# One branch per unit over two written-out sides, in place of one branch per pair of tiles

## What is computed

```python
x = x + _L0_conv_ref(_gn(x), w0, w1, w2, bias)     # wavelet convolution, three levels
x = x + _L1_conv_ref(_gn(x), spatial_weight)       # similarity filter
```

```python
patches = _extract_patches(x)                      # 25 neighbours of each point
dot = jnp.einsum('bchw,bckhw->bkhw', x, patches)
norm_x = jnp.sqrt(jnp.sum(x * x, axis=1))
norm_p = jnp.sqrt(jnp.sum(patches * patches, axis=1))
sim = dot / jnp.maximum(norm_x[:, None] * norm_p, 1e-08)
weight = (sim + 1.0) * 0.5 * spatial_weight[None, :, None, None]
out = jnp.einsum('bckhw,bkhw->bchw', patches, weight)
```

## Time and profile before

| | |
|---|---|
| median of three runs | 2016.01 us |
| the profiled execution: its time / its span | 2011.4 us / 2009.7 us |
| TensorE, matmul busy | 1638.6 us, 82% |
| VectorE busy | 1370.1 us, 68% |
| ScalarE busy | 748.9 us, 37% |
| GpSimd busy | 428.0 us, 21% |
| mean granted TensorE clock | 0.908 |
| one loop iteration (six between first and last L1529 branch) | 225.6 us |

### The profile page before, as it was taken

One profiled execution on the slowest core, in us unless ns is written; L12 is line 12 of the kernel. 1 busy time (PEld: TensorE's weight loads), 2 busy tenths in 40 slices (PEclk: granted clock), 3 DMA queues, 4 the chain that ended last, 5 costly groups with the idle time before them and its releaser, 6 DMA issues.

```text
span 2009.7 us, 52625 instructions
## 1 busy us (share of the span) xinstructions
PE 1638.6 (82%) x19071; PEld 899.9 (45%) x19071; DVE 1370.1 (68%) x1995; ACT 748.9 (37%) x1318; POOL 428.0 (21%) x760
## 2 busy tenths in 40 slices
PE   4868688888888888888888888888888889886587
PEld 3533244444544454444544454444544444443355
DVE  6434956885588756885588656884589666885554
ACT  1321134432444244432544234432444244432551
POOL 2344232212040222212040222212040222210000
PEclk8889889889998999889999889999999998898567
DMA  5233137754475627754575627754575637662665
GB/s 182 84 97 98 52 93 202 199 152 119 131 212 155 155 83 204 195 157 115 133 209 150 154 74 204 201 155 119 134 204 156 154 96 197 188 162 68 163 170 133
DMA packets 108623, 296.77 MB, mean 148 GB/s; under 512 B 24180, under 2 KB 57972, under 8 KB 107764
## 3 DMA queue, kind: packets, MB, share of 16 engines
q1 hardware_dynamic: 71408, 190.49, 36.1%
q0 software_dynamic: 36864, 101.47, 17.5%
HBM read 221.92 MB, written 69.94 MB: 145 GB/s over the span
## 4 chain that ended last, share of the span: by engine, by line
PE 56%; DVE 21%; issue 14%; ACT 4%; DVEq 2%; DMA 1%; POOL 1%; ACTq 0%; SPq 0%; POOLq 0%
PE conv L1272 14%; PE conv L1246 10%; PE gram L1337 7%; PE out_ps L1373 5%; PE stat_ps L1295 5%; PE conv L1231 5%; DVE wgt L1014 3%; PE out_ps L1362 3%; PE vals_ps L1320 3%; DVE st_s L965 2%; DVE eo L830 2%; DVE st_a L962 2%; PE conv L1493 2%; DVE st_v L976 1%; DVE st_b L957 1%
## 5 line engine op out<-in xcount | busy, mean ns | idle before, releaser
L1272 PE MATMUL conv<-thl,wconv 128*128 128x496 f16 (+2 forms) x1920 | 521.7, 398 | 29.5 <-issue 14.9
L1014 DVE SCALAR_TENSOR_TENSOR wgt<-gram,tapw 124x512 f32<-124x512 f32 x512 | 349.7, 685 | 269.0 <-PE gram L1337 232.8
L452 POOL DMA_DIRECT2D ring<-in_x x576 | 331.9, 582 | 354.2 <-ACT xa L524 263.9
L1337 PE MATMUL gram<-unit_mem 128*60 128x128 f16 x4096 | 251.5, 246 | 63.9 <-DVE wgt L1014 32.6
L1337 PEld LDWEIGHTS gram<-unit_mem 128*60 128x60 f16 x4096 | 151.2, 112 | 290.6 <-issue 289.8
L1246 PE MATMUL conv<-thl,wconv 128*128 128x480 f16 (+7 forms) x1200 | 257.7, 369 | 0.0
L1272 PEld LDWEIGHTS conv<-thl,wconv 128*128 128x128 f16 x1920 | 163.6, 101 | 197.8 <-issue 42.0
L481 POOL DMA_DIRECT2D up<-d_z x128 | 69.3, 546 | 666.1 <-DVE xa L945 630.6
L1295 PE MATMUL stat_ps<-st_sq,sq_c 128*128 128x306 f32 x256 | 112.2, 525 | 111.6 <-DVE flag L995 68.9
L524 ACT ACTIVATE vals<-vals_ps 124x512 f32<-124x512 f32 x128 | 76.2, 595 | 308.1 <-PE vals_ps L1320 307.5
L524 ACT ACTIVATE thl<-tw 128x1024 f16<-128x1024 f32 x64 | 67.7, 1058 | 329.1 <-DVE tw L830 184.2
(11 more groups left out here) (140 smaller groups left out, 2114.0 us busy)
## 6 DMA issues: line engine op xcount, KB each, us to landing
unit_mem<-d_hl SPq DMA_DIRECT2D x128, 360.0 KB
unit_mem<-d_hl SPq DMA_DIRECT2D x256, 180.0 KB
ring<-in_x POOLq DMA_DIRECT2D x288, 128.0 KB, 2.7
ring<-in_x POOLq DMA_DIRECT2D x288, 127.0 KB, 2.7
d_hl<-st_hl SPq DMA_DIRECT2D x64, 360.0 KB
d_v<-st_v SPq DMA_DIRECT2D x64, 360.0 KB
unit_mem<-d_v SPq DMA_DIRECT2D x64, 360.0 KB
up<-d_z POOLq DMA_DIRECT2D x160, 128.0 KB, 2.6
```

Of the source, the lines that this page charges most:

```text
L452: pool.dma_start(dst, src).then_inc(raw_in[slot], 16)
L1014: V.scalar_tensor_tensor(out=dst, in0=g, scalar=SIM_SCALE ** 2, in1=tapw[:, :].unsqueeze(1).to_broadcast([KN, 2, 2 * QN]), op0=ALU.add, op ...
L1272: last = mm(dst[:, :, b0:b1], wconv0[:, w, 2 * (p % ROWS4) + s, dx + 2, :], thl[:, p % 2, d, s, :, b0 + dx:b1 + dx] if p % ROWS4 != 1 else ...
L1337: last = mm(bank[row:row + KQ, col:col + QN], key[:, q, e_at, TH * KW * g:TH * KW * g + KQ], tile[:, :, TH * g + 1:TH * g + 1 + TH, 1:1 + ...
```

## The change

On both engines the body of a unit becomes a function `unit(j, guarded)`. In place of a branch in every pair there is one branch after the load of the flag, with the whole unit written out on each side: first the side with the guard in all eight pairs, then the side without any. `Chain.mark` and `Chain.back` let both sides use the same link numbers. On TensorE the wait for the flag and its load stand ahead of `conv_points` now, and so ahead of that function's own waits, where they stood in hook k = 0 behind them.

```diff
-            def weights(b, u, k, short_ones):
+            def weights(b, u, k, guarded):
...
-                with dve.If(short_ones > 0):
-
+                if guarded:
                     V.tensor_scalar(dst, guard_ps[0:KN, :].rearrange("p (t n) -> p t n", t=2), 1 / EPS_SIM, 1.0, ALU.mult, ALU.min)
                     dve.drain()
                     V.tensor_tensor(g, g, dst, ALU.mult)
                     dve.drain()
...
+                for j in range(CONV_TILES):
+                    if ls:
+                        dve.wait_ge(flag_done, START + 8 * b + j + 1)
+                        alone(dve)
+                        short_ones = dve.value_load(flag[0:1, j % FLAGS:j % FLAGS + 1], min_val=0, max_val=P * FN)
+                        chains = gn1_chain, gn2_chain, prep_chain, wino_chain
+                        marks = [chain.mark() for chain in chains]
+                        with dve.If(short_ones > 0):
+                            unit(j, True)
+                        for chain, mark in zip(chains, marks):
+                            chain.back(mark)
+                        with dve.Else():
+                            unit(j, False)
+                    else:
+                        unit(j, False)
...
-            def gram(b, u, k, short_ones):
+            def gram(b, u, k, guarded):
...
-                with pe.If(short_ones > 0):
-
+                if guarded:
                     pe.wait_ge(wgt_done, START + n)
...
                             if k == 0:
-                                pe.wait_ge(flag_done, START + 8 * b + j + 1)
-                                alone(pe)
-                                short_ones[0] = pe.value_load(flag[0:1, j % FLAGS:j % FLAGS + 1], min_val=0, max_val=P * FN)
                                 unit_here(b, j)
...
+                for j in range(CONV_TILES):
+                    if ls:
+                        pe.wait_ge(flag_done, START + 8 * b + j + 1)
+                        alone(pe)
+                        short_ones = pe.value_load(flag[0:1, j % FLAGS:j % FLAGS + 1], min_val=0, max_val=P * FN)
+                        with pe.If(short_ones > 0):
+                            unit(j, True)
+                        with pe.Else():
+                            unit(j, False)
+                    else:
+                        unit(j, False)
```

More of the change, by code:

```diff
@@ L146, in round, with mark, back @@
         self.base, self.k = n * self.per_round, 0
+    def mark(self):
+        return self.base, self.k
+    def back(self, mark):
+        self.base, self.k = mark
     def link(self, engine, instruction):
@@ L1069, in iteration, with unit @@
                     level1_out(i, 1)
-                short_ones = None
-                for j in range(CONV_TILES):
+                def unit(j, guarded):
                     h = j + AHEAD
[L1073 to L1076, removed]
                     for k in range(PAIRS):
@@ L1080, in iteration @@
                                 set_flag(b, 2)
-                            weights(b, j, k, short_ones)
+                            weights(b, j, k, guarded)
                             if k == 0 and j in (2, 3, 4, 5):
@@ L1378, in iteration @@
                 b = i - 1
-                short_ones = [None]
                 if conv_on:
@@ L1425, in iteration, with unit, hook @@
                         hook_1(n)
-                for j in range(CONV_TILES):
-                    def hook(n, j=j):
+                def unit(j, guarded):
+                    def hook(n):
                         if n not in HOOKS:
@@ L1441, in hook @@
                             if k < PAIRS:
-                                gram(b, j, k, short_ones[0])
+                                gram(b, j, k, guarded)
                             if k == 1:
```

## The result

The change takes 2213.24 us in the median of 4 runs (2198.08 to 2225.87), the kernel before 2020.41 (1999.98 to 2024.87, 4 runs). The ratio is 1.0973, with a 95% interval of 1.0869 to 1.1077: slower by some 10%. The forecast was 2140 us with a range of 2030 to 2205. The direction was right, and so was the main mechanism, the far jump of TensorE that has to wait for its target; the loss is 193 us where 129 were forecast, and 2213 lies outside the range. The profiled execution of the change took 2198.08 us, 186.7 more than that of before; what follows is about these 187.

A forecast was written before the change was run, and what follows sets the result against it. TensorE (82% busy) set the pace in units 6, 7 and the last iteration, waiting for VectorE's flag at other starts. Terms 79 + 50 + 40 + 10 - 35 - 15 = +129 on 2011.4 gave 2140 us, range 2030 to 2205.

The forecast's parts named there:

- the first rival: TensorE's jump target is already fetched, so a far jump costs what a pair's branch does: 1961 us; chance 0.08.
- Terms 5 and 6: TensorE's late instruction packets get rarer in denser straight code, -35 us; the removed pair branches save exposed hand-over time, -15 us.
- the fourth rival: Straight code is worth more: all late packets vanish, hand-overs give 46 us, jumps cost 2.5 with slack: 1960 us; chance 0.03.
- Term 8: VectorE's new branch over 69 to 105 instructions: zero cost, covered by TensorE's own jump; uncovered up to 2.5 us a unit.
- term 7: TensorE's flag wait and load (302 ns) moved ahead of `conv_points`' waits: zero, up to 0.3 us a unit where those last.
- The third rival: Both engines pay in turn: VectorE's jump also needs a packet, starting its first pair 2.5 us later: 2230 us; chance 0.05.
- the slack case: VectorE catches up within units 0 to 5 and no clock is lost anew, so only 22 starts count: 2027 us; chance 0.12.
- The packets: Sign in the instruction queue: some 270 packets in all instead of 236, as every unit ends with one fetched and dropped.
- term 2: Units 0 to 5 of seven iterations, 42 starts: TensorE 1.6 us late beyond its existing wait, three quarters counted, +50 us.
- the 3.6 us for every start: Idle added per TensorE far jump, priced like the loop's way back; 22 starts at TensorE's pace made +79 us.
- Term 3: TensorE's clock drops after idle: 14 starts of units 6 and 7 lose 2 us each, 42 others some 0.3; +40 us.
- Term 4: Where the plain side begins near a packet's end, TensorE wants the next at once: two of eight starts, +10 us.

## Why the prediction failed, point by point

**What held.** The target isn't there and has to be fetched: 64 of 64 branches over 3.3 us, so the first rival fell, and with it what I had read out of the 2048 instructions that the Trainium skill's page "Runtime: NRT & Kernel Launch" gives TensorE. In rows: 121 instructions jumped over cost 0.2 to 0.6 us, 401 cost 3.4 to 6.3 in six units of eight, and in one of the other two, unit 7, the same idle came a few instructions behind a short branch. The same section of the Trainium skill, "Instruction fetch mechanics", has blocks of 256 instructions and a stall where the target is outside the current two; the traces agree with it (the rows of before gave about 235 instructions for a packet), and give the price that it leaves open.

**Terms 5 and 6** (late packets -35, removed branches -15): idle by "issue" other than before first products fell by 36 us, and the kernel with short sides is 54 us faster than before, where the two terms had 50 together. Right; the fourth rival had 106 for them. **Term 8** (VectorE's jump 0) and **term 7** (load ahead 0): VectorE's branch is 56 ns in all 64, and the early load by itself moved nothing that can be seen. Right, and not only by the cover that I named for it: with VectorE's sides alone there is no jump of TensorE, and the kernel gains. The third rival is out, and so is the slack case: VectorE's longer waits (+204 us) went with a longer iteration.

**The packets**: 283 for some 270. Right.

**The step that failed is term 2, in unit 0, and with it the 3.6 us for every start.** To see it, the forecast has to be laid out by place. The starts of units 0 to 5 had 1.6 x 3/4 + 0.3 = 1.5 us each, those of units 6 and 7 3.6 + 2 = 5.6, those of the last iteration 3.6; the -40 of terms 4 to 6 spread over 64 units takes 0.6 from each. That makes, in us over the whole run:

| place | forecast | measured |
|---|---|---|
| unit 0, 7 times | 6 | 55 |
| units 1 to 5, 35 times | 30 | 49 |
| units 6 and 7, 14 times | 70 | 58 |
| last iteration, 8 times | 24 | 25 |
| sum | 130 | 187 |

49 of the 57 us missing are in unit 0. Three things were wrong there. It has no 2 us of waiting that could swallow the jump: the prediction took the 1.90 us from the start of unit 4 for all of 0 to 5, while unit 0 of the kernel before has 0.7 us of idle in all (18.70 less 18.01). Its jump isn't 3.6 but 6.9 us, because the packet starts 3.8 to 5.0 us after the branch while data transfers fill the DMA engines (share 0.99). And the 5 us of idle cost the clock for the first half of the unit, 3.3 us of busy time in the mean of the seven, where the forecast had 0.3. The kernel with fewer loads undoes the second, and the third goes with it: of 7.8 us (55 / 7) some 1.4 remain (141.0 less 131.1, over 7; the kernel before with fewer loads has 131.1 too), not far from the 0.9 to 1.5 that I had for a jump of 3.6 us.

Both could be seen in the trace of before. Windows of a loop's end, of the start of a unit 0 and of a unit 6, in the kernel before:

```profile
934.40:939.40 5.00, 0.61 (x17) 0.34 (x16) 2.56 (x4) 0.85 (x2) 0.00 (x0) 0.84 0.34 76
999.20:1003.00 3.80, 3.37 (x25) 1.55 (x23) 0.78 (x2) 0.73 (x1) 0.00 (x0) 1.00 0.98 231
1126.30:1130.00 3.70, 3.41 (x56) 1.54 (x46) 3.27 (x6) 0.69 (x1) 1.37 (x3) 1.00 0.92 227
```

The way back, from which I took the price, falls where the DMA engines have a share of 0.34; the new jumps of units 0 and 6 fall where it is 0.98 and 0.92. And TensorE is busy 3.37 of 3.80 us at the start of unit 0, so nothing there could take a delay. I read one start of each regime and put eight under two names.

**Units 1 to 5** cost 1.4 us each where 0.9 was forecast net: the jumps of 3.6 to 4.0 are as priced, and the wait for the flag, 1.7 to 2.7 us in units 1 to 4, is gone. Unit 5 never had that wait, against what the prediction says of units 1 to 5; its 2.1 us for late packets and 1.5 for the weights vanished instead, and it costs 0.0 us where units 1 to 4 cost 1.3, 1.9, 1.4 and 2.4. The busy time is 0.9 us longer in the mean of these five against the 0.3 of the forecast (by unit +1.6, +1.5, +0.3, +0.8, +0.1). **Units 6 and 7** came under the sum, by opposite errors: unit 6 costs 6.0 us a time, for its jump is 6.0 us and not 3.6; unit 7 costs 2.2 with what follows it. That is two things, in the mean of the six iterations that another follows. Unit 7 itself, from its load to the last matmul before the way back, takes 22.0 us for 17.1, the 5 us that were forecast. But the idle of the way back is 3.5 for 4.2, and the matmuls that follow until unit 0 take 57.0 for 59.6, all of it busy time, at a higher granted clock (before, then the change):

```profile
1168.10:1227.90 59.80, 53.02 (x256) 29.73 (x257) 33.47 (x50) 28.64 (x51) 11.95 (x21) 0.93 0.48 126
1262.70:1319.80 57.10, 50.23 (x254) 28.14 (x255) 33.88 (x50) 28.66 (x51) 11.90 (x21) 0.97 0.49 131
```

Why the clock is higher there no run isolates. **The last iteration** agrees partly by luck: it was not free of waits (13.5 us for the weights, of which 7.5 went), its idle grew by 32 us, and 7 less of busy time bring that down to 25. **Term 3** (clock, +40) against +52 of busy time: near in sum, wrong in place, and so luck: 23 of it are in unit 0, 31 in units 1 to 5 and 9 in unit 6, and unit 7 with what follows and the last iteration have 12 less. The forecast had 28 of its 40 in units 6 and 7. **Term 4** (+10) can't be told from the rest in the change; the kernel with 401 instructions shows what it is.

By kind the same 187 us are: +269 idle before first products, -69 waits for the flag, -24 waits for the weights net, -36 late packets, +52 busy, -5 the rest and rounding. The idle that the new one replaced is the idle that the prediction had read as waits, and little on top.

## What to carry to other kernels

A few far branches may cost more than many near ones: on TensorE a jump past what has been fetched took 3.4 to 4 us, forward or back, with a condition or without, and 6 to 7 with the DMA engines full, where a near one took 0.2 and mostly hid. A short branch record alone doesn't make a jump near: look at the idle before the next matmuls as well. So count the instructions that each branch jumps over, and write out the sides on an engine where they are short (here VectorE). Price a stall place by place: by the slack at that start, the DMA share at that time, and the clock that the idle takes.

## What the runs showed of the hardware

- TensorE's far branch consists of 0.94 to 1.55 us until the packet starts, 0.9 to 1.4 for the packet, and 1.35 to 1.6 until the next instruction (units 1, 3, 4 and 5 of the change). With full DMA engines the first part is 2.5 to 5.0 us.
- The same distance of 401 instructions gives a record of 3.4 to 4.1 us, or of 0.45 to 1.1, depending on the unit's place in the program (units 0 and 6 aside), in every iteration of the loop alike. Where it was 0.45, TensorE stood all the same: the packet behind the target was missing, and the first products came after 3.3 to 4.2 us of idle.
- The 5 us of idle in unit 0 cost TensorE 3.3 us more of busy time in the mean, 4.3 in the unit shown, at a clock of 0.81; after 1.67 us of idle at the same place the clock stayed 1.00. No limit follows from this: at the start of unit 4 the four matmuls were slow after 1.90 us too.
- VectorE jumped over 69 to 105 instructions in 56 ns, 64 times of 64.
